# Flamingo block with routed experts: another order of loads, projections, maxima and dense tiles, keys in chunks of 128, and the maxima's rows sent from ScalarE's queue

## The reference

```python
q = LN(x) @ Wq + bq          # 8 x 112 x 256, 16 heads of 16
k, v = ctx @ Wk + bk, ctx @ Wv + bv      # 8 x 375 x 192 -> 256
attn = softmax(q k^T / 4); o = (attn v) @ Wo + bo
x = x + tanh(g_xattn) * o
logits = LN(x) @ wg; e = argmax; gate = max softmax       # 8 experts
# each expert takes the first 112 tokens that chose it, in order
x = x + tanh(g_ffn) * gate * (LN(x) @ W[e]^T + b[e])      # 0 for the others
```

## Time and profile before

| | us |
|---|---|
| median of 3 runs | 228.31 |
| the three runs | 226.72, 228.31, 231.46 |
| the profiled execution | 226.61 |
| its span, first to last instruction | 224.8 |
| PE busy in it | 184.9 (82%) |
| DVE, ACT, POOL busy | 123.7, 91.5, 94.3 |
| chain that ended last, by engine | PE 66%, DVE 13%, DMA 8%, POOL 5% |
| mean granted TensorE clock | 0.922 of 2.4 GHz |

### The profile page before, as it was taken

How to read it: one execution, slowest core, us unless ns; L and a number is a source line. 1 busy time by engine, 2 the same in 40 slices (tenths; PEclk the granted TensorE clock), 3 DMA queues, 4 the chain that set the end, 5 groups by cost and what they waited for, 6 DMA issues and landing times.

```text
span 224.8 us, 4335 instructions
## 1 busy us (share of the span) xinstructions
PE 184.9 (82%) x1692; PEld 111.7 (50%) x1692; DVE 123.7 (55%) x292; ACT 91.5 (41%) x200; POOL 94.3 (42%) x145
## 2 busy tenths in 40 slices
PE   0866869743999899899899989989989896479990
PEld 0342426412556466557556646646656563257640
DVE  7037465563454855754764675485585436254651
ACT  0262243231374365456527527544636654021200
POOL 5632639779245056038037235413022553103730
PEclk9999599995699999999999999999999998556998
DMA  6968049999940910840660490180351233560110
GB/s 187 264 156 169 0 107 291 226 238 294 291 139 16 224 65 5 191 109 3 142 162 0 100 203 3 40 171 0 94 146 57 69 113 116 155 175 28 57 51 20
DMA packets 17660, 27.40 MB, mean 122 GB/s; under 512 B 4007, under 2 KB 12817, under 8 KB 17272
## 3 DMA queue, kind: packets, MB, share of 16 engines
q1 hardware_dynamic: 15176, 23.82, 41.6%
q0 software_dynamic: 944, 2.28, 3.3%
q10 hardware_dynamic: 1520, 1.03, 1.9%
HBM read 10.03 MB, written 5.29 MB: 68 GB/s over the span
## 4 chain that ended last, share of the span: by engine, by line
PE 66%; DVE 13%; DMA 8%; POOL 5%; ACT 2%; issue 2%; ACTq 1%; SPq 1%; DVEq 0%
PE stp L476 14%; PE pv L491 12%; PE sc L465 8%; PE misc L522 4%; PE stp L407 4%; DMA bv_sb<-in_bv 4%; DVE nmax L809 4%; PE pj L423 3%; PE pj L439 3%; PE misc L580 2%; DVE pvT L816 2%; DMA k<-parts_k 2%; DMA q<-mrows 2%; PE pj L444 2%; PE pv L580 2%
## 5 line engine op out<-in xcount | busy, mean ns | idle before, releaser
L809 DVE TENSOR_REDUCE nmax<-sc 112x1 f32<-112x375 f32 x128 | 68.2, 543 | 54.6 <-PE sc L465 53.8
L733 ACT ACTIVATE prob<-stp 125x448 f32<-125x448 f32 x96 | 52.2, 544 | 61.2 <-PE stp L476 60.8
L465 PE MATMUL sc<-k,q 128*112 128x375 bf16 x128 | 41.8, 343 | 9.1 <-DVE nmax L809 6.7
L476 PE MATMUL stp<-q,k 128*125 128x112 bf16 x384 | 42.8, 236 | 3.2 <-DMA q<-mrows 3.2
L491 PE MATMUL pv<-prob,v_sb 125*32 125x112 f32 x768 | 38.7, 273 | 2.1 <-issue 1.3
L476 PEld LDWEIGHTS stp<-q,k 128*125 128x125 bf16 x384 | 30.3, 140 | 20.1 <-issue 16.5
L491 PEld LDWEIGHTS pv<-prob,v_sb 125*32 125x32 f32 x768 | 15.4, 108 | 23.6 <-ACT prob L733 10.1
L1000 POOL TENSOR_SCALAR ve<-mv 112x1 f32<-112x1 f32 x8 | 1.9, 233 | 57.4 <-DVE mv L838 57.4
L465 PEld LDWEIGHTS sc<-k,q 128*112 128x112 bf16 x128 | 17.2, 135 | 16.4 <-DVE nmax L809 11.4
L423 PE MATMUL pj<-ctx_sb,wk_sb 128*128 128x375 f32 x32 | 15.4, 580 | 7.8 <-DMA ctx_sb<-in_ctx 7.8
L1017 POOL TENSOR_TENSOR kf<-kf,parts_k 128x375 f32<-128x375 f32 x14 | 12.6, 899 | 19.1 <-ACT kf L677 19.1
(11 more groups left out here) (125 smaller groups left out, 240.7 us busy)
## 6 DMA issues: line engine op xcount, KB each, us to landing
k<-parts_k SPq DMA_DIRECT2D x48, 187.5 KB, 3.8
ctx_sb<-in_ctx SPq DMA_DIRECT2D x2, 1125.0 KB, 7.6
early<-in_wT SPq DMA_DIRECT2D x8, 256.0 KB, 4.3
slots<-empty SPq DMA_DIRECT2D x8, 224.9 KB, 4.6
ctx_sb<-slots SPq DMA_DIRECT2D x8, 224.9 KB, 4.5
q<-parts_q SPq DMA_DIRECT2D x6, 224.0 KB, 3.7
q<-parts_q SPq DMA_DIRECT2D x6, 168.0 KB, 3.7
k<-in_be SPq DMA_DIRECT2D x1, 896.0 KB, 5.1
```

What stands on the lines that cost most here:

```text
L465: pe.matmul(sc[h % 2][0:NQ, 0:NK], q_heads(b)[:, h, :], k6[:, b % KR, h, :], start=True, stop=True).then_inc(s_sc, 1)
L476: mm = pe.matmul(stp[n % 2][0:KN, j * NQ:(j + 1) * NQ], k6[:, b % KR, h, c * KN:(c + 1) * KN], q_heads(b)[:, h, :], start=True, stop=True)
L733: nc.scalar.activation(prob[0:KN, n % 3, :], stp[n % 2][0:KN, 0:4 * NQ], ACT.Exp, scale=SCALE).then_inc(s_p, 1)
L809: nc.vector.tensor_reduce(nmax[:, b % 2, h:h + 1], sc[h % 2][0:NQ, 0:NK], axis=AX.X, op=ALU.max, negate=True).then_inc(s_max, 1)
```

## The change

- **Loads.** wk moves from SP's queue to ACT's, behind x of tile 0 and the biases of q, k and v, which are now one array and one DMA; wo, bo and wg move from ACT's queue to SP's, to step 14. The context comes in five loads (tiles 0, 1, 2, 3, 4 to 7) in place of four, x in 1, 2 and 5 tiles in place of 1, 4 and 3.
- **Projections.** q is projected in four groups (tile 0; 1, 2; 3 to 5; 6, 7). K of tile 1 and the second group of q are projected before the steps begin (which now begin at 0). ACT zeroes two groups of q and loads its activation table early; two layer norms go to POOL; the bv product moves to step 20.
- **Maxima.** `HEADS` has two heads in each of steps 0 to 4 and none in step 6. Split, turn and transfer are at 12, 13, 14. `normalise_pv` is cut into three steps (30, 31, 32), Wo is at 33, `add_x` at 34, layer norm at 36, logits at 39.
- **The maxima's rows** are sent from ACT's queue (`act.dma_start`, behind a wait for ACT's own copy), not from SP's.
- **Chunks.** Keys are cut 128, 128, 119 in place of 125, 125, 125. `scores_T` reads 128 columns of k as weights in every chunk (k has 16 columns more at its end for that), and V's chunks follow.
- **Dense tiles.** Tile 6 too isn't gathered. Its dense products are put between the steps of the last tile's end, those of tile 7 come after the experts.

The core of the diff:

```diff
-NCH = 3
-KN = NK // NCH
+CHUNKS = [(0, 128), (128, 128), (256, NK - 256)]
-HEADS = ((0, 1), (2,), (3,), (4, 5), (6,), (7,), (8, 9), (10,), (11,), (12, 13), (14,), (15,))
+HEADS = ((0, 1), (2, 3), (4, 5), (6, 7), (8, 9), (10,), (), (11,), (12,), (13,), (14,), (15,))
-SPLITMAX_AT, MAXT_AT, MROW_AT = 13, 14, 15
+SPLITMAX_AT, MAXT_AT, MROW_AT = 12, 13, 14
-NORM_AT, WO_AT, ADD_AT = 30, 31, 32
-LN_AT, X2T_AT, LG_AT = 33, 35, 36
+NORM_AT, WO_AT, ADD_AT = (30, 31, 32), 33, 34
+LN_AT, X2T_AT, LG_AT = 36, 38, 39
-QG = ((0, 1), (1, 5), (5, 8))
+QG = ((0, 1), (1, 3), (3, 6), (6, 8))
...
@@ SP
-            sp.dma_start(wk_sb[:, :, :], wk).then_inc(s_wk, 16)
             load_ctx(0, 0, 1)
-            sp.dma_start(x_sb[:, 1:5, :], x[:, 1:5, :]).then_inc(s_x[1], 16)
+            sp.dma_start(x_sb[:, 1:3, :], x[:, 1:3, :]).then_inc(s_x[1], 16)
             load_ctx(1, 1, 2)
-            sp.dma_start(x_sb[:, 5:B, :], x[:, 5:B, :]).then_inc(s_x[2], 16)
+            sp.dma_start(x_sb[:, 3:B, :], x[:, 3:B, :]).then_inc(s_x[2], 16)
             lay_k(0)
             lay_q(0)
-            for s in range(FIRST, LAST + 1):
-                if s == 1:
-                    lay_q(1)
-                    load_ctx(2, 2, 5)
-                if found := at(s, MROW_AT, 1):
-                    b, _ = found
-                    sp.wait_ge(s_mrows, b + 1)
-                    sp.dma_start(q_heads(b)[MAXROW:MAXROW + 3 * STEP:STEP, :, :], mrows[:, :])\
-                      .then_inc(s_mrow, 16)
+            lay_k(1)
+            load_ctx(2, 2, 3)
+            lay_q(1)
+            for s in range(END):
+                if s == MROW_AT:
+                    load_ctx(3, 3, 4)
+                    sp.dma_start(wo_sb[:, :, :], wo).then_inc(s_wo, 16)
...
+                    lay_q(2)
+                    load_ctx(4, 4, 8)
...
@@ PE
             def scores_T(b, n):
...
-                    mm = pe.matmul(stp[n % 2][0:KN, j * NQ:(j + 1) * NQ],
-                                   k6[:, b % KR, h, c * KN:(c + 1) * KN], q_heads(b)[:, h, :],
+                    k0 = h * NK + CHUNKS[c][0]
+                    mm = pe.matmul(stp[n % 2][:, j * NQ:(j + 1) * NQ],
+                                   k6_flat[:, b % KR, k0:k0 + 128], q_heads(b)[:, h, :],
...
@@ PE, after the loop
             pe.wait_ge(s_wT, 16 * E)
+            dense(0, 0)
+            places(1, GATHERED, GATHERED + 1)
+            through_wo(B - 1)
+            turn_share(0)
+            dense(0, 1)
+            choose_bias(0)
+            turn_xn2(B - 1)
             turn_xin(0)
-            places(2, *R2)
-            for e in range(1, E):
+            logits(B - 1)
+            dense(0, 2)
+            places(2, B - 1, B)
+            dense(0, 3)
+            turn_xin(1)
+            pe.wait_ge(s_lge, B)
+            product(0)
+            turn_share(1)
+            for e in range(2, E):
                 turn_xin(e)
                 product(e - 1)
+                if e == 2:
+                    pe.wait_ge(s_counted, 1)
+                    choose_bias(1)
             product(E - 1)
...
+            for p in range(4):
+                dense(1, p)
...
@@ ACT
+                if found := at(s, MROW_AT, 1):
+                    b, _ = found
+                    act.wait_ge(s_mrows, b + 1)
+                    act.dma_start(q_heads(b)[MAXROW:MAXROW + 3 * STEP:STEP, :, :], mrows[:, :])\
+                       .then_inc(s_mrow, 16)
...
@@ DVE
+                if found := at(s, NORM_AT[0], 1):
+                    turn_pv(found[0])
+                if found := at(s, NORM_AT[1], 1):
+                    divide(found[0])
+                if found := at(s, NORM_AT[2], 1):
+                    turn_back(found[0])
...
+            route(1, GATHERED, GATHERED + 1)
+            turn_pv(B - 1)
+            divide(B - 1)
+            turn_back(B - 1)
+            weigh(0)
+            add_x(B - 1)
+            normalise_2(B - 1)
+            take_bias(0)
+            add_dense(0, 0)
+            route(2, B - 1, B)
+            add_dense(0, 1)
+            weigh(1)
+            add_dense(0, 2)
+            add_dense(0, 3)
```

## The result

The change makes the kernel slower. Over 20 runs of each the median is 231.33 us (229.44 to 233.98) after the change and 228.03 us (223.71 to 231.46) before it; the ratio is 1.023, 95% interval 1.0186 to 1.0274, so it is slower, and by about 2%. The profiled execution of the changed kernel has a span of 229.3 us against 224.8, at a mean granted clock of 0.932. I had predicted 212.2. One of the profiles used further down, that of the kernel called POOL's order, is of a slower run of its kernel (226.4 us, where its fast runs took 221.8 to 223.2).

The account below looks back on a forecast made before the run. The prediction took PE (TensorE) to bound the middle. Its terms, -5.0 + 1.0 - 2.3 - 5.7 - 0.3 + 0.5 - 2.6 = -14.4, brought the profiled 226.6 us to 212.2, range 206 to 219.

Parts of the forecast that it names:

- turn 0: Twelve steps running tile 0's transposed scores: the bv product through Wo moves in from the start, plus 1.0 us.
- The start: Before the first transposed score: new load and projection order brings that score from 54.6 to 49.6 us, minus 5.0.
- Rival D: Start: first transfer no earlier, with four context tiles in flight beside it and POOL late; 216.2 us, chance 0.06.
- The boundary: Between tiles: cutting the DVE stretch into three steps shortens PE's wait from 0.99 to 0.6 us, six times, minus 2.3.
- The wide load: Transposed scores: 128-wide weight loads cut load-matmul spacing from 73 to 56 ns, minus 5.7 us in turns 0 to 6.
- rival B: Transposed scores: the weight load is hidden wholly, pairs at 49 ns; 210.1 us, chance 0.20.
- Rival A: Transposed scores: the 128-wide load is no faster, as in f32, so 6.0 us fall away; 218.2 us, chance 0.17.
- ACT's issue: Each turn: sending the maxima's rows from ACT's queue takes 0.78 us there, mostly hidden, plus 0.5 us in all.
- Rival C: Each turn: the issue on ACT delays the exponential in all eight turns; 217.9 us, chance 0.05.
- The tail: From the last pv group to the end: tile 6 also dense, 33.0 us in place of 35.6, minus 2.6.
- Rival E: Tail: PE falls to half clock and stays there, plus 22 us; 234 us, chance 0.02.
- Turn 7: Last tile's turn, bound by a loop: transposed-score group 0.05 us shorter in 1.4, minus 0.3 us.

Follow-up runs that it names:

- POOL's order: Changed kernel with the maxima's split, turn and transfer one step later and the layer norm one step earlier, before the K split: ratio 0.989 to the kernel before.
- the three edits together: Changed kernel with x's bias addition one tile a turn, context of tiles 4 to 7 loaded at step 18, and POOL's order: ratio 0.952 to the kernel before.
- the best one here: The three edits together, with the turn of xn2 and the logits one step later for tiles 0 to 5: 214.88 us against 227.46 before, ratio 0.943.

## Why the prediction was wrong, point by point

Three terms failed: the first transfer from issue to use (4.1 us assumed, 8.66 measured), turn 0 (plus 0.2 assumed, plus 7.1 measured), and the middle turns (minus 1.2 each assumed, plus 0.5 measured).

**The start: the step from issue to use failed.** The walk to the issue was good: first maximum predicted at 25.3, measured 24.85; issue predicted at 45.5, measured 44.41. I had started PE at 7.0, and it was 9.00; the start had slack for it. Then I gave the transfer 4.1 us "on its own queue beside a load of four tiles", and it took 8.66. The experiment with the load later gives 2.87. I took the other queue for a reason to expect less delay than the earlier trace rows shows, with a larger load beside it; that was the wrong sign. The start's own bound of minus 1, "the transfer then waits for the larger load", was close to the minus 1.5 measured. Rival D named this mechanism, at a chance of 0.06 and with POOL late as a second condition; POOL wasn't needed.

The Trainium skill, "DMA: Bandwidth & Descriptors", section "Queues, rings and completion order", says that each DMA engine goes round the queues that have work, packet by packet. By that alone one would expect a small transfer on a queue of its own to pass a large one. The trace doesn't bear this out: 10.5 KB on ACT's queue took 8.66 us beside SP's 1,500 KB, and 2.87 without them. The same section says that the increment of the semaphore, by which a transfer reports, lands only after every earlier write of that DMA engine, across its queues. That would let one expect a delay, and the trace agrees in the direction; no run here separates it from the DMA engines simply being full.

**Turn 0: a part of a moved step was not counted.** I costed the move of the bv product at plus 1.0 for its four PE instructions. What follows from it on POOL I left out: the addition to x, which in the kernel before ran at 51.73 us while nothing waited for POOL, lands 8.6 us later, in the middle of turn 0, in front of the split of tile 1's maxima. Its length was there to be read, from POOL's own stream: 4.50 us in the kernel before. Spreading it gives back 6.0. The prediction's PE part, 1.0, is inside what remains (19.81 against 18.6 of a later turn).

**The middle turn: two terms right, one left out.** The boundary: 0.99 to 0.6 predicted, 0.61 measured. The number is right and its reason is not: the wait ends on ACT's exponential (behind an eviction of V), not on DVE's first transpose, which starts at 116.16 and ends 0.1 us earlier. The wide load: 0.82 predicted, 0.64 measured. Its spacing fell to (0.37 - 0.213) / 3 = 52 ns, even lower than my 56, from 73; but only three spacings in a group of four are saved, not four: 12 x 3 x 21 ns = 0.76, of which 0.12 are still missing in the measurement and not placed. So rival B's size of the spacing was closer, and the count was the mis-sized term. What I left out is the order of POOL's work. I followed DVE, ACT and PE through the new steps, and took POOL, at 40%, to be free. With the maxima a step earlier and the layer norm at step 36, its chain delivers just too late, twice a turn. The order alone costs 0.92 a turn with 125 columns (19.08 against 18.16) and 1.11 with 128 (18.63 against 17.52). The longer idle time explains 0.35 and 0.55 of that. The rest, 0.57 and 0.56, is busy time of PE with the same instructions, as the three windows above show. When the waits for POOL and for the turned maxima are gone, busy time falls by 0.29 too (17.02 to 16.73), which fits a wait that costs more than the idle time in its row; the steps moved for it may have a part in that. What holds the other 0.27 in the new order was not shown.

**The Trainium skill's rule on wide loads** ("TensorE: Matmul & The Clock Gate", section "Weight-path perf modes — Fast Weight Load (FWL) and DoubleRow") holds here: at 128 bf16 columns the load takes 98 ns, at 125 it takes 137. That is 1.4 times as fast, where the page says about twice. Rival A, that it would be no faster, is refuted.

**ACT's issue: nothing, where I took 0.5.** The issues take 0.73 us each (1.36 the first), no wait of PE in the middle turns ends on them, and turns 1 to 7 are as long with the rows on SP's queue. Rival C is refuted.

**The tail: close.** 33.0 predicted; 33.7 in the changed kernel, 32.2 where all of it ran at full clock. Rival E is there in small: from 191.5 to 197.5 us the clock is 0.50, the first dense product takes 3.36 us where it has 1.97 at full clock, which is nearly all of the difference. The clock is back at full from about 198.5 us, and PE works almost without a gap. The sign that I named, a clock above 0.9 all through the tail, failed; no more than 1.5 us hang on it.

**Turn 7:** plus 1.8 in place of minus 0.3. 2.1 us of it go by the chip, as shown; on the first one it was 11.3, minus 0.2.

Of the 18.9 us between forecast and result the three edits together give back 16.7 (230.1 to 213.4 us of span, on one chip). The forecast was a kernel in which nothing is late, 210.4 us of span; the best one here, at 211.7, comes close to it. It isn't the kernel of the forecast, though: its middle turns (17.36 against 17.0) are longer, and its transfer (3.4 us against 4.1) is shorter. What made the chance of 0.93 wrong is that each loss needed only one unchecked queue: SP's bytes in flight, and POOL's position in one step.

## What to carry to other kernels

When a step is moved, list what every engine does because of it, and for each piece the next thing queued behind it; an engine that is busy 40% of the time still holds PE up if two of its deliveries fall due in the same microsecond. In this kernel a small transfer on the critical path took three times as long with a large load ahead of it, though that was on another queue: issue the large, patient load after it, and check who is next behind that load. Price a faster weight load by the spacings between matmuls that it shortens (here three in a group of four) and test it alone; it was worth 2.3% by itself and was buried by the order that came with it.

## What the runs showed of the hardware

- A bf16 weight load of 128 by 128 takes 98 ns, one of 128 by 125 takes 137; f32 loads don't differ. All loads of the transposed scores 128 wide, the last chunk's of 119 keys among them, are a gain of 0.64 us a turn; the last chunk alone was not tested.
- A transfer of 10.5 KB on one queue took 8.66 us behind 1,500 KB issued 4 us earlier on another, and 2.87 us without them; six transfers of 187.5 KB on the other queue stood beside it both times. The large load itself had landed 7.7 us after its issue, before the small one.
- In turn 0 a wait of 4.62 us in place of 0.73 cost 6.0: PE's clock was granted at 0.50 after it, with PE fully busy. In the last turn, waits of 0.3 to 0.8 us, one or two microseconds apart, were followed by the same, in one kernel for 6 us.
- The last turn of the same kernel took 11.34 us on one chip and 13.42 on another, with ACT's exponentials starting late and nothing in the trace to name for it.
